# Adding the window mask with VectorE instead of a mask matmul, in a kernel of causal attention and six local-attention layers

## The chip, the cores and the metric

The kernel runs on one core of one Trainium2 chip. The metric is the device time of one execution in microseconds. PE is TensorE (PEld its weight loads), DVE is VectorE, ACT is ScalarE, POOL is GpSimd, SP the queue that issues the DMAs. A matmul writes into one of eight banks of PSUM (here `ps[0]` to `ps[7]`); DVE and ACT read the banks, POOL works in SBUF ("memory" below) alone.

## The reference, cut to what matters

A causal attention block is followed by six layers of local attention, each with a feed-forward block. The change touches only the softmax of the local attention, 8 batches of 512 tokens with 16 heads of 64 columns, in windows of 32 queries that look at 64 keys:

```python
sim = jnp.einsum('bhwie,bhwje->bhwij', bq, bk2) * QK_SCALE
sim = jnp.where(mask, -jnp.finfo(sim.dtype).max, sim)
attn = jax.nn.softmax(sim, -1)
out = jnp.einsum('bhwij,bhwje->bhwie', attn, bv2)
```

The mask depends on the position in the window, and it is another one for the first window of a sequence, which has no window before it.

## The kernel before

Every engine has its own instruction stream, written out by hand; they meet only at semaphores. The causal block comes first. Then each engine loops over the six layers. A layer's local attention runs over 32 tiles of 128 tokens (4 in each of 8 batches) as a software pipeline: `pipeline` calls `step` for t from 0 on, and in one step the parts of the work belong to different tiles, `lag` steps behind the newest (projection, squares and rotation lag 0, the transposes of q and k lag 1, scores and softmax lag 2, the transposed probabilities lag 3, weighing lag 3 and 4, the output projection up to lag 6). The feed-forward block follows after the last tile has drained.

A step has two halves, `wp` = 0 and 1. In a half the engines do, each strictly in this order:

- PE: `project(2wp)`, `turn_qk(2wp)`, `turn_p(wp)`, `project(2wp+1)`, `score(wp)`, in half 0 `windows`, then `weigh`, `turn_qk(2wp+1)`, `project_out`.
- ACT: `square(2wp)` (L777), `turned_qk(2wp)` and `turned_p(wp)` (copies, L668), `square(2wp+1)`, in half 0 two small copies, `weighed` (two copies), `turned_qk(2wp+1)`, `exp(wp)` (L820), `norms(wp)` (L786, L789, L793, which end with `rn`).
- DVE: `sums` (L1129, L1131), `rotate(2wp)` and `rotate(2wp+1)` (L1093), `shift(wp)` (L1116, L1119), two `square_sums` (L1105), then one of `update` and `rests_of_tile` (half 0) or `load_next` (half 1).
- POOL: two `scale` (L1311), `normalise` (L1320), two `add` (L1297).

What holds a half together: `rotate(c)` waits for `square(c)`; `add(c)` waits for `rotate(c)`; `norms` waits for the second `square_sums`; the first `square` of the next half stands behind `norms` in ACT's order; `scale` waits for `rn`. A tile of scores (128 x 512, the bank `sbank`) is made by 16 small matmuls of `score`. Ahead of them stands one matmul that puts the mask there: `identb` (the unit matrix) times `lmask`, both bfloat16, 128 x 512, and the scores are accumulated on top. `score` also waits until `shift` of the half before has read the bank for the last time (semaphore `sub`). `shift` takes the maximum of each head's 64 scores from the bank (L1116), waits for it, and subtracts it while it moves the scores to memory, into `dd` (L1119). `exp` works in place on `dd`.

Of the kernel before, what the change touches and what calls it, by code (L numbers as in the profile page):

```python
# [22 lines left out]
ALU = mybir.AluOpType  # L23
AX = mybir.AxisListType

P = 128
# [4 lines left out]
DEPTH, D, WIN = 6, 64, 32  # L31
HP = HEADS // 2
# [57 lines left out]
def build(nc, ins, out, layers=DEPTH):  # L90
    ctx = ExitStack()
    with ctx:
        def sb(name, shape, dt=F32):
            return ctx.enter_context(nc.sbuf_tensor("sb_" + name, [P] + shape, dt))

        def sem(name):
            return ctx.enter_context(nc.semaphore("s_" + name))
# [9 lines left out]
        identb = sb("identb", [P], BF16)  # L107
        lmask = sb("lmask", [2, HP * 2 * WIN], BF16)
# [21 lines left out]
        smax, ssum, srec = sb("smax", [2, HP]), sb("ssum", [2, HP]), sb("srec", [2, HP])  # L130
# [4 lines left out]
        def take(*shape):  # L135
            n = int(np.prod(shape))
            v = area[:, at[0]:at[0] + n]
            at[0] += n
            if len(shape) == 1:
                return v  # L140
            names = " ".join("abcde"[:len(shape)])
            return v.rearrange(f"p ({names}) -> p {names}", **dict(zip("abcde", shape)))
# [4 lines left out]
        dd, pT = take(2, 512), take(2, 512)  # L147
# [3 lines left out]
        kT = take(HP, WIN + T)  # L151
# [48 lines left out]
        def ea(h, qt, k0, k1):  # L200
# [7 lines left out]
        pj, rbank, sbank, tbank, ybank, mbank = ps[0:2], ps[2], ps[3], ps[4], ps[5:7], ps[7]  # L208

        S = {n: sem(n) for n in (  # L210

            "const", "xload0", "xload1", "xload2", "xload3", "c_weights", "eps_set", "v16_zero", "wo_zero", "w_loaded", "w_loaded2", "w1_loaded", "w2_loaded",
            "wcomb_mm", "wcomb_ready",

            "ln0_mean", "ln0_sq", "ln0_rstd", "ln0_x", "xn_tr", "xT_ready", "xs_zero",

            "xb_ready", "c_proj", "c_rope", "c_rope_part", "v_mm", "v_ready", "qm_ready", "c_score", "c_max",
            "c_exp", "c_split", "stack0", "stack1", "stack2", "stack3", "c_rec", "c_p", "c_tr", "c_ptev", "c_pv", "yT_ready", "ca_mm", "res_in", "ca_sum", "ca_out",

            "kT_zero", "w_split", "w_split_h", "w_split_a", "rots_ready", "wvo_mm", "wvo_ready", "xs_part", "xs_high", "xs_ready",  # L220
            "proj", "sq", "rotd", "ssq", "ssq_raw", "guard_set", "ln_part", "rn", "add", "qn", "tr", "ev", "score",
            "smax", "sub", "exp", "ssum", "srec", "pn", "pt", "ptev", "yy", "yev0", "yev1",
            "xwt", "xwev", "oo", "xupd",

            "lx", "lx_zero", "lmean", "ldif", "lsq", "lvar", "lln", "lrs", "lmul", "xn", "mhi", "mlo", "gate", "gelu", "aa",
# [17 lines left out]
        def behind(t, i, part, lag):  # L243

            s = t - lag
            if (part == 0 and s < 0) or (part == 2 and s >= 2 * TT):
                return None
            return s % TT, i + s // TT
# [106 lines left out]
        def _(pe):  # L355
            def mm(o, a, b, start=True, stop=True):
                return nc.tensor.matmul(o, a, b, start=start, stop=stop, skip_group_check=True)  # L357
# [84 lines left out]
            with pe.Fori(0, layers) as l:  # L442
# [14 lines left out]
                def step(t, i, part):  # L457
                    def g_of(bt):
                        return l * B + bt
# [47 lines left out]
                    def score(wp):  # L507
                        if not (v := behind(t, i, part, 2)):
                            return
                        tt, bt = v  # L510
                        pe.wait_ge(S["ev"], g_of(bt) * 16 + 4 * tt + 4)
                        pe.wait_ge(S["sub"], g_of(bt) * 8 + 2 * tt + wp)
                        first = tt == 0 and wp == 0
                        mm(sbank[:, :], identb[:, :], lmask[:, 0 if first else 1, :], True, False)
                        for g in range(HP):
                            for x in range(2):
                                hp, w = 2 * (g // 2) + x, wp + 2 * (g % 2)
                                k0 = tt * P + w * WIN
                                m = mm(sbank[64 * x:64 * x + 64, g * 64:(g + 1) * 64],
                                       qbd[:, tt % 2, hp, w, :, :].rearrange("p a b -> p (a b)"),  # L520
                                       kT[:, hp, k0:k0 + 2 * WIN], False, x == 1 and g == HP - 1)
                        m.then_inc(S["score"], 1)

                    def turn_p(wp):
# [66 lines left out]
                    for wp in range(2):  # L591
                        project(2 * wp)
                        turn_qk(2 * wp)
                        turn_p(wp)
                        project(2 * wp + 1)
                        score(wp)
                        if wp == 0:
                            windows()
                        weigh(4 - wp, 1 - wp)
                        turn_qk(2 * wp + 1)  # L600
                        project_out(wp)
# [327 lines left out]
        def _(dve):  # L929
            tt_, ts_ = nc.vector.tensor_tensor, nc.vector.tensor_scalar  # L930

            def bc(v, shape, axis):
                return v.unsqueeze(axis).to_broadcast(shape)
# [113 lines left out]
            with dve.Fori(0, layers) as l:  # L1047
# [28 lines left out]
                def step(t, i, part):  # L1076
                    def g_of(bt):
                        return l * B + bt
# [30 lines left out]
                    def shift(wp):  # L1109
                        if not (v := behind(t, i, part, 2)):  # L1110
                            return
                        tt, bt = v
                        m_ = g_of(bt) * 8 + 2 * tt + wp
                        dve.wait_ge(S["score"], m_ + 3)
                        s3 = sbank[:, :].rearrange("p (h k) -> p h k", h=HP)
                        nc.vector.tensor_reduce(smax[:, wp, :], s3, AX.X, ALU.max).then_inc(S["smax"], 1)  # L1116
                        dve.wait_ge(S["smax"], m_ + 1)
                        dve.wait_ge(S["pt"], m_ + 1)
                        tt_(dd[:, wp, :].rearrange("p (h k) -> p h k", h=HP), s3,  # L1119
                            bc(smax[:, wp, :], [P, HP, 64], 2), ALU.subtract).then_inc(S["sub"], 1)  # L1120

                    def sums(lag, wp):
                        if not (v := behind(t, i, part, lag)):
# [36 lines left out]
                    for wp in range(2):  # L1160
                        sums(3 - wp, 1 - wp)
                        rotate(2 * wp)
                        rotate(2 * wp + 1)
                        shift(wp)
                        square_sums(2 * wp)
                        square_sums(2 * wp + 1)
                        if wp == 0:
                            update()
                            if not (part == 0 and t == 0) and (v := behind(t, i, part, -1)):
                                rests_of_tile(*v)  # L1170
                        else:
                            load_next()
# [216 lines left out]
```

## Time and profile before

| | us |
|---|---|
| median of 3 runs (4154.02 to 4157.87) | 4154.56 |
| the profiled execution | 4155.47 |
| its span, first to last instruction | 4153.7 |
| busy: PE / PEld / DVE / ACT / POOL | 3814.5 / 2939.8 / 3258.6 / 3109.2 / 2498.3 |
| share of the span | 92% / 71% / 78% / 75% / 60% |
| mean granted TensorE clock | 0.971 of 2.4 GHz |

A matmul's end is modelled, so that a PE that is 92% busy isn't at its peak. The causal block fills the first 700 us, and the six layers take some 570 us each. In the last part of a layer, the feed-forward block, nothing of the change runs. A share over the whole span mixes these stages; the rows below are therefore read stage by stage.

### The profile page before, as it was taken

How to read it: one execution, taken by the hardware profiler on the slowest of the kernel's cores; microseconds unless marked ns; L12 is line 12 of the kernel's file. 1: busy time of each engine (PE TensorE's matmuls, PEld its weight loads, DVE VectorE, ACT ScalarE, POOL GpSimd, SP SyncE). 2: the span in 40 equal slices, each digit the busy share in tenths (PEclk: the TensorE clock that was granted, in tenths of full speed). 3: DMA queues.
4: the chain of work that ended last, by engine and by line, in shares of the span. 5: the costliest groups of instructions: out<-in, count | busy, mean ns of one | idle time of the engine just before them, and what ended most of it. 6: DMA issues, size and time to landing. Idle time of an engine off the chain costs nothing.

```text
span 4153.7 us, 101302 instructions
## 1 busy us (share of the span) xinstructions
PE 3814.5 (92%) x30950; PEld 2939.8 (71%) x31328; DVE 3258.6 (78%) x5635; ACT 3109.2 (75%) x7150; POOL 2498.3 (60%) x2247
## 2 busy tenths in 40 slices
PE   6999998899998999988999989999889999899998
PEld 4666665677766777766777667777667776677776
DVE  5877876888867888768888678887688886788876
ACT  4777776788866888857888668887578886688875
POOL 1221221777745777737777457776377774577763
PEclk9999999999998999998999989999989999999999
DMA  2111111000010000010000100000100000000002
GB/s 79 42 32 31 29 39 35 2 0 0 0 28 1 1 0 0 1 28 1 0 0 0 28 1 1 0 0 1 28 1 0 0 0 28 1 1 0 0 1 68
DMA packets 53261, 52.86 MB, mean 13 GB/s; under 512 B 13574, under 2 KB 40452, under 8 KB 51972
## 3 DMA queue, kind: packets, MB, share of 16 engines
q1 hardware_dynamic: 52996, 49.77, 4.5%
q8 instruction: 113, 1.85, 0.2%
q14 instruction: 152, 1.25, 0.1%
HBM read 28.77 MB, written 4.19 MB: 8 GB/s over the span
## 4 chain that ended last, share of the span: by engine, by line
issue 26%; PE 24%; ACT 24%; DVE 21%; ACTq 2%; DVEq 2%; POOL 1%; SPq 0%; DMA 0%; POOLq 0%
PE bank L357 19%; ACT sb_area L668 12%; DVE sb_ssq L1105 10%; DVE sb_smax L1116 6%; ACT sb_area L777 5%; PE bank L416 3%; ACT sb_lnb L786 3%; ACT sb_lnb L789 3%; DVE sb_area L1093 1%; PE bank L503 1%; POOL sb_area L1336 1%; DVE sb_nmx L1013 1%; DVE sb_area L1119 0%; PE bank L532 0%; DVE sb_area L1009 0%
## 5 line engine op out<-in xcount | busy, mean ns | idle before, releaser
L668 ACT ACTIVATE sb_area<-bank 128x512 f32<-128x512 f32 (+4 forms) x3029 | 1570.3, 553 | 259.0 <-PE bank L357 182.3
L357 PE MATMUL bank<-sb_area 128*64 128x64 f32 (+4 forms) x16624 | 1286.1, 274 | 94.9 <-issue 57.8
L1093 DVE TENSOR_TENSOR sb_area<-bank,sb_rots 128x1024 f32<-128x1024 f32 x768 | 939.2, 1224 | 395.2 <-ACT sb_area L777 394.4
L1311 POOL TENSOR_TENSOR sb_area<-sb_area,sb_rn 128x512 f32<-128x512 f32 x768 | 784.8, 1043 | 608.5 <-ACT sb_rn L793 608.5
L1297 POOL TENSOR_TENSOR sb_area<-sb_area 128x512 f32<-128x512 f32 x768 | 967.9, 1278 | 78.3 <-DVE sb_area L1093 76.2
L357 PEld LDWEIGHTS bank<-sb_area 128*64 128x64 f32 (+2 forms) x16624 | 849.5, 151 | 200.6 <-issue 139.1
L357 PE MATMUL bank<-sb_wqk_hi,sb_xwin 128*128 128x512 f32 x1536 | 729.7, 477 | 53.9 <-DVE sb_xwin L1073 43.6
L357 PE MATMUL bank<-sb_area,sb_wvo 128*128 128x256 f32 x3072 | 728.3, 381 | 3.1 <-DVE sb_xT L1151 3.1
L357 PEld LDWEIGHTS bank<-sb_area,sb_wvo 128*128 128x128 f32 x3072 | 555.0, 190 | 78.3 <-issue 12.8
L503 PE MATMUL bank<-sb_ident,sb_area 128*128 128x128 f32 x3072 | 494.9, 285 | 33.4 <-ACT sb_area L668 31.0
L503 PEld LDWEIGHTS bank<-sb_ident,sb_area 128*128 128x128 f32 x3072 | 358.8, 144 | 227.6 <-issue 160.0
L1105 DVE TENSOR_REDUCE sb_ssq<-sb_area 128x8 f32<-128x512 f32 x768 | 486.7, 675 | 0.0
L777 ACT ACTIVATE sb_area<-bank 128x512 f32<-128x512 f32 x768 | 460.4, 600 | 30.9 <-PE bank L357 14.5
L1320 POOL TENSOR_TENSOR sb_area<-sb_area,sb_srec 128x512 f32<-128x512 f32 x384 | 400.3, 1042 | 88.4 <-DVE sb_srec L1131 88.4
L1270 POOL TENSOR_TENSOR sb_ptT<-sb_xwin,sb_hm 128x512 fp32r<-128x512 f32 x128 | 137.8, 1077 | 510.8 <-PE bank L357 494.1
L722 ACT ACTIVATE sb_area<-bank,sb_nmx 128x128 f32<-128x128 f32 (+3 forms) x512 | 270.1, 528 | 178.5 <-DVE sb_nmx L1013 175.6
L357 PEld LDWEIGHTS bank<-sb_wqk_hi,sb_xwin 128*128 128x128 f32 x1536 | 304.2, 198 | 111.3 <-issue 48.9
L1013 DVE TENSOR_REDUCE sb_nmx<-bank 128x1 f32<-128x128 f32 (+3 forms) x512 | 249.1, 487 | 125.4 <-PE bank L357 114.4
L357 PE MATMUL bank<-sb_wqk_lo,sb_xwin 128*128 128x512 f32 x768 | 315.4, 411 | 0.0
L820 ACT ACTIVATE sb_area<-sb_area 128x512 f32<-128x512 f32 x384 | 242.9, 633 | 76.4 <-DVE sb_area L1119 70.9
L357 PE MATMUL bank<-sb_xwin,sb_ptT 128*128 128x128 f32 (+3 forms) x512 | 286.9, 561 | 13.3 <-POOL sb_ptT L1270 8.4
L1129 DVE TENSOR_REDUCE sb_ssum<-sb_area 128x8 f32<-128x512 f32 x384 | 261.6, 681 | 45.2 <-ACT sb_area L820 40.0
(103 smaller groups left out, 4861.7 us busy)
## 6 DMA issues: line engine op xcount, KB each, us to landing
sb_xwin<-sb_p SPq DMA_DIRECT2D x256, 64.0 KB, 2.0
sb_area<-in_Wqkv SPq DMA_DIRECT2D x7, 1024.0 KB, 5.8
sb_area<-in_WvT SPq DMA_DIRECT2D x7, 512.0 KB, 7.3
sb_wo_bd<-in_Wo SPq DMA_DIRECT2D x14, 256.0 KB, 8.2
sb_area<-in_x SPq DMA_DIRECT2D x4, 512.0 KB, 5.7
sb_area<-in_x SPq DMA_DIRECT2D x8, 256.0 KB, 2.9
x_plus_causal<-sb_area SPq DMA_DIRECT2D x8, 256.0 KB, 2.3
out<-sb_area SPq DMA_DIRECT2D x8, 256.0 KB, 3.5
```

Source lines behind the costliest of these rows:

```text
L357: return nc.tensor.matmul(o, a, b, start=start, stop=stop, skip_group_check=True)
L503: m = nc.tensor.transpose(rbank[:, j * P:(j + 1) * P], qn[:, c, j * P:(j + 1) * P], ident[:, :])
L668: return nc.scalar.activation(o, i, ACT.Copy)
L722: nc.scalar.activation(ea(k // TT, qt, 0, (qt + 1) * P), ps[k % 3][:, 0:(qt + 1) * P], ACT.Exp, bias=nmx[:, k % 8:k % 8 + 1], accum_out=ls ...
L777: nc.scalar.activation(sqb[:, c % 2, :], pj[c % 2][:, :], ACT.Square).then_inc(S["sq"], 1)
L1013: nc.vector.tensor_reduce(nmx[:, k % 8:k % 8 + 1], ps[k % 3][:, 0:(k % TT + 1) * P], AX.X, ALU.max, negate=True).then_inc(S["c_max"], 1)
L1093: tt_(t12[:, c % 2, :, :].rearrange("p u (h d) -> p u h d", h=8), src, bc(rots[:, tt, s, :, :], [P, 2, 8, D], 2), ALU.mult).then_inc(S["ro ...
L1105: nc.vector.tensor_reduce(ssq[:, tt % 2, half, 8 * (c % 2):8 * (c % 2) + 8], sqb[:, c % 2, :].rearrange("p (h d) -> p h d", h=8), AX.X, AL ...
L1129: nc.vector.tensor_reduce(ssum[:, wp, :], d3, AX.X, ALU.add).then_inc(S["ssum"], 1)
L1297: pt_(qsum[:, c % 2, :].rearrange("p (h e d) -> p h e d", h=8, e=2), t12[:, c % 2, 0, :].rearrange("p (h e d) -> p h e d", h=8, e=2), swap ...
L1311: pt_(qn[:, c, :].rearrange("p (h d) -> p h d", h=8), qsum[:, c % 2, :].rearrange("p (h d) -> p h d", h=8), r, ALU.mult).then_inc(S["qn"], 1)
L1320: pt_(dd[:, wp, :].rearrange("p (h k) -> p h k", h=HP), dd[:, wp, :].rearrange("p (h k) -> p h k", h=HP), srec[:, wp, :].unsqueeze(2).to_b ...
```

## The change

The mask matmul goes, and the first score matmul of each 64 x 64 block starts its own accumulation. `shift` now has three operations of 128 x 512 elements in place of two. The first adds `lmask` (bfloat16, memory) to the bank and writes `dd` (float32, memory). The maximum is taken from `dd`, and the subtraction reads `dd` and writes `dd`. The wait for `pt` (that `dd`'s old content was transposed) comes ahead of the first of them. `score` waits for the new semaphore `masked` instead of `sub`.

```diff
@@ score (PE)
-                        pe.wait_ge(S["sub"], g_of(bt) * 8 + 2 * tt + wp)
-                        first = tt == 0 and wp == 0
-                        mm(sbank[:, :], identb[:, :], lmask[:, 0 if first else 1, :], True, False)
+                        pe.wait_ge(S["masked"], g_of(bt) * 8 + 2 * tt + wp)
...
                                        qbd[:, tt % 2, hp, w, :, :].rearrange("p a b -> p (a b)"),
-                                       kT[:, hp, k0:k0 + 2 * WIN], False, x == 1 and g == HP - 1)
+                                       kT[:, hp, k0:k0 + 2 * WIN])
@@ shift (DVE)
                         dve.wait_ge(S["score"], m_ + 3)
-                        s3 = sbank[:, :].rearrange("p (h k) -> p h k", h=HP)
-                        nc.vector.tensor_reduce(smax[:, wp, :], s3, AX.X, ALU.max).then_inc(S["smax"], 1)
+                        dve.wait_ge(S["pt"], m_ + 1)
+                        tt_(dd[:, wp, :], sbank[:, :], lmask[:, 0 if tt == 0 and wp == 0 else 1, :], ALU.add)\
+                            .then_inc(S["masked"], 1)
+                        dve.wait_ge(S["masked"], m_ + 1)
+                        d3 = dd[:, wp, :].rearrange("p (h k) -> p h k", h=HP)
+                        nc.vector.tensor_reduce(smax[:, wp, :], d3, AX.X, ALU.max).then_inc(S["smax"], 1)
                         dve.wait_ge(S["smax"], m_ + 1)
-                        dve.wait_ge(S["pt"], m_ + 1)
-                        tt_(dd[:, wp, :].rearrange("p (h k) -> p h k", h=HP), s3,
-                            bc(smax[:, wp, :], [P, HP, 64], 2), ALU.subtract).then_inc(S["sub"], 1)
+                        tt_(d3, d3, bc(smax[:, wp, :], [P, HP, 64], 2), ALU.subtract).then_inc(S["sub"], 1)
```

## Rows read from the trace of the kernel before

**Rows 1.** Chain of waits, two halves of the second layer: start, us, engine, line.

```profile
1403.49 0.69 DVE sb_smax L1116
...
1410.99 0.69 DVE sb_smax L1116
1411.70 0.06 DVE sb_area L1119
...
1412.31 1.28 DVE sb_ssq L1105 x2
...
1414.29 0.04 ACT sb_rn L793
...
1415.03 1.08 ACT sb_area L668 x2
1416.11 0.50 ACT sb_area L777
...
1417.77 0.69 DVE sb_smax L1116
```

**Rows 2.** Who waited for whom, 760 to 1176 us: us, times, longest.

```profile
DVE sb_area L1093 <- ACT sb_area L777: 56.9, 116, 1.1
ACT sb_lnb L786 <- DVE sb_ssq L1105: 29.4, 58, 0.6
...
ACT sb_area L668 <- PE bank L357: 21.1, 34, 0.9
```

**Rows 3.** Busy time by stretch: length, PE, PEld, DVE, ACT, POOL, granted clock, DMA.

```profile
760.00:1176.00 416.00, 397.24 (x3834) 321.35 (x3891) 353.79 (x562) 342.92 (x751) 320.44 (x292) 1.00 0.00 1
1304.00:1324.00 20.00, 13.08 (x79) 9.51 (x81) 14.28 (x19) 12.93 (x31) 16.20 (x15) 0.74 0.00 1
1180.00:1210.00 30.00, 28.53 (x247) 21.96 (x245) 9.74 (x18) 16.51 (x31) 6.92 (x7) 1.00 0.01 1
...
220.00:240.00 20.00, 16.42 (x100) 11.11 (x98) 14.58 (x37) 15.63 (x51) 4.16 (x4) 1.00 0.08 21
```

**Rows 4.** Timeline, DVE: first and last maximum of layer one's full pipeline.

```profile
753.58 0.68 DVE L1116 TENSOR_REDUCE sb_smax<-bank 128x8 f32<-128x512 f32 x1
...
1176.12 0.68 DVE L1116 TENSOR_REDUCE sb_smax<-bank 128x8 f32<-128x512 f32 x1
```

**Rows 5.** Lines by themselves: min/median/max ns, first and last start.

```profile
L1119 DVE TENSOR_TENSOR sb_area<-bank,sb_smax x384: 690/691/693, 754.3 to 4049.1; 128x512 f32<-128x512 f32 x192
L1116 DVE TENSOR_REDUCE sb_smax<-bank x384: 678/680/694, 753.6 to 4048.4; 128x8 f32<-128x512 f32 x192
L1129 DVE TENSOR_REDUCE sb_ssum<-sb_area x384: 672/681/687, 756.3 to 4051.1; 128x8 f32<-128x512 f32 x192
L1093 DVE TENSOR_TENSOR sb_area<-bank,sb_rots x768: 1211/1224/1226, 728.0 to 4026.5; 128x1024 f32<-128x1024 f32 x192
L984 DVE TENSOR_TENSOR sb_area<-sb_area x16: 680/682/693, 47.8 to 594.2; 128x512 f32<-128x512 f32 x16
L1219 DVE TENSOR_TENSOR sb_p<-sb_area,sb_p x36: 691/692/1466, 1244.6 to 4127.2; 128x512 fp32r<-128x512 f32 x36
```

**Rows 6.** Timeline, PEld: the mask's weights and the first ones of the scores.

```profile
1407.39 0.10 PEld L357 LDWEIGHTS bank<-sb_lmask,sb_identb 128*128 128x128 bf16 x1 [0.27 <-issue]
1407.72 1.01 PEld L357 LDWEIGHTS bank<-sb_area 128*64 128x64 f32 x32 [0.23 <-issue]
```

**Rows 7.** Timeline, DVE and POOL, feed-forward block: a lengthened operation and its surroundings.

```profile
1243.22 2.32 POOL L1343 TENSOR_TENSOR sb_xwin<-sb_area,sb_xwin 128x512 fp32r<-128x512 f32 x2 [6.12 <-ACT sb_xwin L668]
...
1244.62 1.46 DVE L1219 TENSOR_TENSOR sb_p<-sb_area,sb_p 128x512 fp32r<-128x512 f32 x1
```

**Rows 8.** Timeline, POOL: the two adds of half 0 and of half 1.

```profile
1410.09 2.51 POOL L1297 TENSOR_TENSOR sb_area<-sb_area 128x512 f32<-128x512 f32 x2
...
1417.59 2.52 POOL L1297 TENSOR_TENSOR sb_area<-sb_area 128x512 f32<-128x512 f32 x2
```

**Rows 9.** Timeline, DVE: a maximum while the pipeline drains.

```profile
1192.13 0.69 DVE L1116 TENSOR_REDUCE sb_smax<-bank 128x8 f32<-128x512 f32 x1 [1.02 <-PE bank L357]
```

More of the change, by code:

```diff
@@ L221, in build @@
             "proj", "sq", "rotd", "ssq", "ssq_raw", "guard_set", "ln_part", "rn", "add", "qn", "tr", "ev", "score",
-            "smax", "sub", "exp", "ssum", "srec", "pn", "pt", "ptev", "yy", "yev0", "yev1",
+            "masked", "smax", "sub", "exp", "ssum", "srec", "pn", "pt", "ptev", "yy", "yev0", "yev1",
             "xwt", "xwev", "oo", "xupd",
```

## The prediction

> **What bounds the kernel now.** The change lies in the local attention alone, so I looked for that stage first, and in it for the resource whose lengthening lengthens a half. The busy shares point at PE: in the full pipeline of the first layer it is busy for 397.24 of 416 us, against 353.79 for DVE [rows 3]. A matmul's end is modelled, though, so I went on to the chain of waits. There a half runs through DVE and ACT alone [rows 1]: maximum at 1410.99, subtraction at 1411.70, the square sums at 1412.31, ACT's three norm operations ending with `rn` (starts 1414.29), the first square, two copies (1415.03), the second square (1416.11), the second rotation, and the next maximum at 1417.77. This is a closed loop: DVE waits for the square, ACT waits for the square sums. Third, the waits confirm it [rows 2]: in the 416 us DVE waits 56.9 us for the square (116 times, about twice per half), and ACT waits 29.4 us for the square sums (58 times, once per half). ACT also waits 21.1 us for PE, 34 times, but that is for the weighed values, which stand ahead of its wait for the square sums, so there is slack behind it. No row has the loop waiting for the scores in steady state.
>
> A half lasts 7.50 us (1403.49 to 1410.99) or 6.78 us (1410.99 to 1417.77), 14.28 for a step [rows 1]. As a check over the stage: 60 maxima, the first at 753.58 and the last at 1176.12, give 422.54/59 = 7.16 us [rows 4]. The 60 are the halves of steps that still have new tiles; with six layers there are 360 such halves (180 steps), and 24 more (4 a layer) while the pipeline drains, 384 in all, the count of L1116 [rows 5].
>
> **The change part by part.**
>
> *The mask matmul goes.* From its weights (1407.39) to the first ones of the scores (1407.72) it takes 0.33 us of PE's queue [rows 6]. PE isn't in the loop, so in the 360 full halves this is worth 0; it merely gives PE some room. In the drain it is otherwise: PE is busy for 28.53 of 30 us, DVE for 9.74 [rows 3], and the maximum there waits 1.02 us for PE [rows 9]. There PE sets the pace. I count 18 of the 24 halves (the first of a layer's four still hangs on the loop) with 0.33 us, about -6 us. The bounds are -8 (24 x 0.33) and +17 (24 x 0.71, if DVE's new operation shows after all).
>
> *One more DVE operation (add).* It reads the bank and memory and writes 128 x 512 float32, which is L1119's form, 691 ns [rows 5]. The bfloat16 operand is the one difference and no row has it; I take the same time. The maximum has to wait for its result, and the nearest pair of that kind is maximum and subtraction, 0.71 us from start to start (1410.99 to 1411.70) [rows 1]. So the loop grows by 0.71 us in each half. Nothing hides it: it stands between rotation and square sums, both in the loop. The wait for `pt`, moved ahead, costs nothing, since in PE's order `turn_p` stands before `score`. The early release of the bank through `masked` is worth nothing either, as `score` doesn't wait for it. Behind DVE's new wait for `masked` stands only work that needed the maximum, or follows it, already.
>
> *Maximum and subtraction from memory.* The maximum costs the same: 680 ns from the bank (L1116) and 681 from memory (L1129) [rows 5]. The subtraction by itself is 691 ns from bank and memory (L1119) and 682 from memory twice (L984). That would be 0.01 us gained, taken as 0.
> The Trainium skill would expect more from this part: VectorE: DVE Perf Modes, "The TRN2 errata", has a fixed 120 cycles of 0.96 GHz for a bank source and 58 for memory. An estimate from that page is 62 cycles, 0.065 us, for each of two operations in 360 halves, 47 us less. The rows of this case differ (1 and 9 ns).
>
> *But the subtraction now has two operands in memory, and POOL is at work then.* This is the part that decides the size. In the feed-forward block L1219, with two operands in memory, takes 691 ns at best and 692 in the median but 1466 at most [rows 5]. The long one starts at 1244.62 while POOL has two operations from 1243.22 to 1245.54 [rows 7]. It lasts 1.46 us and so ends at 1246.08, 0.54 us behind POOL. Read as one mechanism: such an operation does its first 0.15 us or so (0.69 - 0.54), then stands until POOL's running operation is over, and then takes its 0.54. Operations with one operand in the bank never do so: L1119 (690 to 693 ns) and L1093 (1211 to 1226 ns) keep their time in all their executions [rows 5], though the maximum at 1410.99 and L1119 behind it lie right under POOL's adds. Nor does the reduction from memory (L1129, 672 to 687).
> Where does the new subtraction fall? It starts at the old maximum's place plus twice 0.71. In half 0: 1410.99 + 1.42 = 1412.41, and POOL's adds end at 1410.09 + 2.51 = 1412.60 [rows 1, 8]. Stall: 0.19 - 0.15, 0.04 us. In half 1: 1417.77 + 1.42 = 1419.19, and the adds end at 1417.59 + 2.52 = 1420.11. Stall: 0.92 - 0.15, 0.77 us. POOL's sequence of five operations starts when `rn` is done and is over 5.8 us after `rn`'s start (1414.29 to 1420.11), so a longer loop doesn't move it against DVE: the stall comes back in each step. Together 0.81 us a step.
> The Trainium skill says the same in its GPSIMD Engine Reference, "Specifications": the SBUF interfaces are shared with VectorE, with contention for DVE instructions that have two SBUF inputs. This rule speaks against the change, and the trace agrees, by the 1466 ns above.
>
> *Sum.* Per step 14.28 + 2 x 0.71 + 0.81 = 16.51 us, that is 2.23 more; 180 steps make +401. With the drain's -6 it is +395, on the profiled execution's 4155.5: 4550 us. That execution stands 0.9 us above the median, so against the median the forecast is 4549; I give 4550.
>
> **The rivals.**
>
> *A: no stall.* The subtraction's second operand is only 8 values per partition, each repeated 64 times, and no row shows such an operation beside a busy POOL. If it is exempt, only the add remains: 360 x 0.71 - 6 = +250, 4405 us. For it: that gap in the rows, and that L1219 is stretched in few of its 36 executions (median 692), although few of them need have met POOL. Against it: the full second of POOL ahead of it in half 1.
>
> *B: PE loses its clock and becomes the bound.* PE's work per step is 397.24/416 of 14.28 us, less 0.66 for the two mask matmuls: 13.0 us, while the step grows to 16.5, so it is busy for four fifths. In the filling pipeline, where it was busy for 13.08 of 20 us, the granted clock was 0.74, a mixture of its two levels 1.2 and 2.4 GHz; in the causal block with 16.42 of 20 it was 1.00 [rows 3]. The new state lies near the second. PE would decide from a mean clock of 13.0/16.5 = 0.79 downwards; at 0.74 a step would take 13.0/0.74 = 17.6 us, and the whole 4155.5 + 180 x (17.6 - 14.28) = 4753 us. Against it: a slower clock makes PE busier again. Single dips are taken up by the slack.
> The Trainium skill, TensorE: Matmul & The Clock Gate, Part 1, also has a clock that follows how busy PE was.
>
> *C: not slower, since PE is the real bound.* The mechanism: PE, 95% busy, has no more slack than the loop, and the loop has at least 0.71 us of slack in a half that the chain of waits doesn't show. Then the add disappears and the matmul's 0.33 us come off all 384 halves: -127, 4029 us. It decides from a slack of 0.71 + 0.33 us a half. Against it: a chain that passes from DVE to ACT and back with handovers of some 0.05 us, and scores that are never waited for in the steady state.
>
> **How the numbers follow.** Forecast 4550 us with 0.73; A (4405) 0.15; B and other growth above 4640 0.07; C 0.04; 0.01 for something between. The forecast's own range is 4500 to 4620: it goes up by 54 us if the subtraction needs its full 0.69 us after POOL in every half (360 x 0.15), and down by the estimate that the operations from memory are a little faster or the stall in half 1 is partly missed. To leave out no more than 2 in 10, the range has to reach A: 4395 to 4640. That leaves out B and C, 0.11, and the tails of the rest. 0.2% (8 us) is about what a measurement can tell from no change. Faster by more than that: C, 0.03; within it 0.01, a loop slack that just takes up the add; slower 0.96.
>
> **What the profile would show.** Right: the mean of L1119's successor well above 0.69 us, in two groups (near 0.7 in one half, near 1.45 in the other); the add near 0.69; the step at 16.5 us; POOL's adds ending just as the long subtractions go on; PE's busy share in the stage near 80%, clock near 1; the chain still in DVE and ACT. A: all subtractions 0.68 to 0.69, step 15.7. B: clock of the stage under 0.85 and PE in the chain. C: a step of 14 us with maxima that wait for PE. The forecast would be wrong if the subtraction slipped between POOL's two adds, or if POOL's own operations were held by it and pushed on what waits for them.

## The result and the profile after

The changed kernel takes 4582.11 us (median of 4 runs, 4580.28 to 4583.36) against 4156.22 us for the kernel before (4 runs): the ratio is 1.1024, with a 95% interval of 1.1005 to 1.1043. It is 426 us slower; +395 was forecast. The profiled execution of the changed kernel has a span of 4580.6 us.

First the changed lines by themselves (min/median/max ns, first and last start). L1114 is the add, L1118 the maximum, L1120 the subtraction:

```profile
L1114 DVE TENSOR_TENSOR sb_area<-bank,sb_lmask x384: 650/681/692, 755.3 to 4475.6; 128x512 f32<-128x512 f32 x192
...
L1118 DVE TENSOR_REDUCE sb_smax<-sb_area x384: 686/686/690, 756.0 to 4476.3; 128x8 f32<-128x512 f32 x192
...
L1120 DVE TENSOR_TENSOR sb_area<-sb_area,sb_smax x384: 691/818/1795, 756.7 to 4477.0; 128x512 f32<-128x512 f32 x192
```

Add and maximum take about what was expected, 681 ns for the add instead of 691 and 686 for the maximum instead of 681. The subtraction, 690 to 693 ns before [rows 5], now goes up to 1795. The timeline of one step shows which ones (start, us, engine, line). Half 0 first, then half 1:

```profile
1495.68 2.53 POOL L1297 TENSOR_TENSOR sb_area<-sb_area 128x512 f32<-128x512 f32 x2
...
1498.01 0.74 DVE L1120 TENSOR_TENSOR sb_area<-sb_area,sb_smax 128x512 f32<-128x512 f32 x1
...
1503.96 2.51 POOL L1297 TENSOR_TENSOR sb_area<-sb_area 128x512 f32<-128x512 f32 x2
...
1504.14 0.68 DVE L1114 TENSOR_TENSOR sb_area<-bank,sb_lmask 128x512 f32<-128x512 f32 x1
...
1504.86 0.69 DVE L1118 TENSOR_REDUCE sb_smax<-sb_area 128x8 f32<-128x512 f32 x1
...
1505.58 1.44 DVE L1120 TENSOR_TENSOR sb_area<-sb_area,sb_smax 128x512 f32<-128x512 f32 x1
```

In half 0 POOL's adds end at 1498.21, and the subtraction ends at 1498.75, 0.54 us later. In half 1 they end at 1506.47, and the subtraction, which starts at 1505.58, ends at 1507.02, 0.55 us later. L1219 had shown 0.54 us in the feed-forward block before [rows 7]. This isn't one step alone: 274 of the 384 subtractions take more than 0.72 us, and each of them ends 0.55 us behind an operation of POOL. From the start of the add to that of the maximum, and from there to the subtraction, it is 0.72 us each in half 1.

The chain of waits of the same stretch (start, us, what) is the old loop with the add in it; the 0.83 us of "issue" stand for the held subtraction:

```profile
1504.14 0.69 DVE sb_area L1114
...
1506.11 0.83 issue
1506.94 1.28 DVE sb_ssq L1103 x2
1508.24 0.32 ACT sb_lnb L784
...
1513.02 0.69 DVE sb_area L1114
```

Busy time in the full pipeline (columns as in [rows 3]), to be held against its first line:

```profile
760.00:1176.00 416.00, 361.79 (x3286) 286.30 (x3288) 359.38 (x535) 294.57 (x648) 275.66 (x251) 0.93 0.00 0
```

PE is down from 397.24 to 361.79 us and its clock from 1.00 to 0.93. It now waits for ACT's copy ahead of the window transposes, as one line of the waits of that stretch says (us in total, times, longest). Before, the time of this wait was 7.0 us there.

```profile
PEld bank L559 <- ACT sb_area L666: 54.6, 23, 4.4
```

Where the 426 us are: I took the start of every subtraction. In the full pipeline of a layer, 60 of them now lie 8.31 us apart in the mean (8.30 to 8.32 over the six layers); before it was 7.16 in each. That is 6 x 59 x 1.15 = 407 us. From the last full one to the layer's last one (the drain, four halves) it took 20.75 us before and now takes 22.9 to 24.3 us, together +16 us. The rest, 3 us, is spread.

### The profile page after: what moved, and what is told of

Same layout as the page of the kernel before. It is cut to its first block, busy times and chain, and to the rows that moved or that the text cites. A ratio compares the mean times of both kernels' runs of the same rounds, so it can differ in the third digit from the quotient of the medians.

```text
span 4580.6 us, 101212 instructions
## 1 busy us (share of the span) xinstructions
PE 3957.4 (86%) x30944; PEld 3010.4 (66%) x30944; DVE 3667.2 (80%) x6019; ACT 3108.0 (68%) x7150; POOL 2501.5 (55%) x2247
## 4 chain that ended last, share of the span: by engine, by line
PE 30%; issue 24%; DVE 22%; ACT 18%; DVEq 1%; ACTq 1%; POOL 1%; SPq 0%; DMA 0%; POOLq 0%
PE bank L357 24%; DVE sb_ssq L1103 9%; ACT sb_area L666 9%; DVE sb_smax L1118 4%; DVE sb_area L1114 4%; ACT sb_area L775 4%; PE bank L416 3%; PE bank L503 2%; ACT sb_lnb L787 2%; ACT sb_lnb L784 2%; POOL sb_area L1336 1%; DVE sb_area L1091 1%; PE bank L559 1%; DVE sb_nmx L1011 1%; PE bank L530 1%
## 5 line engine op out<-in xcount | busy, mean ns | idle before, releaser
L357 PE MATMUL bank<-sb_area 128*64 128x64 f32 (+4 forms) x16624 | 1344.8, 282 | 33.3 <-ACT sb_area L666 19.9
L357 PEld LDWEIGHTS bank<-sb_area 128*64 128x64 f32 (+2 forms) x16624 | 878.1, 155 | 262.0 <-issue 180.9
L357 PE MATMUL bank<-sb_area,sb_wvo 128*128 128x256 f32 x3072 | 782.5, 401 | 3.1 <-DVE sb_xT L1151 3.1
L357 PE MATMUL bank<-sb_wqk_hi,sb_xwin 128*128 128x512 f32 x1536 | 732.7, 478 | 57.9 <-DVE sb_xwin L1071 43.8
L357 PEld LDWEIGHTS bank<-sb_area,sb_wvo 128*128 128x128 f32 x3072 | 600.1, 206 | 93.5 <-issue 12.8
L503 PE MATMUL bank<-sb_ident,sb_area 128*128 128x128 f32 x3072 | 532.9, 301 | 27.8 <-ACT sb_area L666 19.3
L503 PEld LDWEIGHTS bank<-sb_ident,sb_area 128*128 128x128 f32 x3072 | 384.1, 152 | 246.9 <-issue 175.4
L559 PE MATMUL bank<-sb_ident,sb_xs 128*128 128x128 f32 x384 | 95.9, 337 | 403.4 <-ACT sb_area L666 403.4
L1120 DVE TENSOR_TENSOR sb_area<-sb_area,sb_smax 128x512 f32<-128x512 f32 x384 | 404.0, 1052 | 13.3
L357 PEld LDWEIGHTS bank<-sb_wqk_hi,sb_xwin 128*128 128x128 f32 x1536 | 305.7, 199 | 116.2 <-issue 49.9
L559 PEld LDWEIGHTS bank<-sb_ident,sb_xs 128*128 128x128 f32 x384 | 42.3, 154 | 431.4 <-ACT sb_area L666 430.4
```

The source lines that it names most:

```text
L503: m = nc.tensor.transpose(rbank[:, j * P:(j + 1) * P], qn[:, c, j * P:(j + 1) * P], ident[:, :])
L1120: tt_(d3, d3, bc(smax[:, wp, :], [P, HP, 64], 2), ALU.subtract).then_inc(S["sub"], 1)
```

## The experiments

Ratios are against the kernel before, from runs on the same chip. It took 4155.7 to 4157.4 us there, so that times of different runs can be compared to about 2 us.

**One: the operands back in the bank.** The add writes into the bank, and what follows reads it there:

```diff
-                        tt_(dd[:, wp, :], sbank[:, :], lmask[...], ALU.add).then_inc(S["masked"], 1)
+                        tt_(sbank[:, :], sbank[:, :], lmask[...], ALU.add).then_inc(S["masked"], 1)
...
-                        nc.vector.tensor_reduce(smax[:, wp, :], d3, AX.X, ALU.max).then_inc(S["smax"], 1)
+                        nc.vector.tensor_reduce(smax[:, wp, :], s3, AX.X, ALU.max).then_inc(S["smax"], 1)
...
-                        tt_(d3, d3, bc(smax[:, wp, :], [P, HP, 64], 2), ALU.subtract).then_inc(S["sub"], 1)
+                        tt_(d3, s3, bc(smax[:, wp, :], [P, HP, 64], 2), ALU.subtract).then_inc(S["sub"], 1)
```

(`s3` is the bank; `score` waits for `sub` again.)

> The changed kernel, but the add writes its result back into the bank, and the maximum and the subtraction read the bank: three operations on VectorE as before, each with one operand in the bank. Theory (the subtraction is held by GpSimd because both its operands are in memory): the subtraction returns to 0.69 us in both halves, the stall of 0.75 us a step goes, 4582 - 180 x 0.75 = 4447 us. Rival (the length of the subtraction has to do with its place in the order, not with where its operands lie): it stays long, 4582 us.

Measured: 4423.78 us (4422.59 to 4425.89), ratio 1.0642 (1.0624 to 1.066). The add costs 267 us with no stall, and putting the subtraction's operand in memory another 158. That is more than the 135 in the expectation: the stall was 0.84 us a step rather than 0.75 (see below), and the drain gets shorter too, to 20.84 us in five of the six layers. The subtraction and the add by themselves:

```profile
L1121 DVE TENSOR_TENSOR sb_area<-bank,sb_smax x384: 690/691/693, 755.5 to 4316.6; 128x512 f32<-128x512 f32 x192
...
L1114 DVE TENSOR_TENSOR bank<-bank,sb_lmask x384: 673/690/700, 754.0 to 4315.1; 128x512 f32<-128x512 f32 x192
```

POOL's adds (1488.42 to 1490.93) run over this subtraction too, in the step below, and leave its length alone:

```profile
1488.42 2.51 POOL L1298 TENSOR_TENSOR sb_area<-sb_area 128x512 f32<-128x512 f32 x2
...
1490.05 0.69 DVE L1121 TENSOR_TENSOR sb_area<-bank,sb_smax 128x512 f32<-128x512 f32 x1
```

**Two: the same collision taken away from POOL's side.** VectorE is as in the changed kernel; the adds take a quarter of the columns, 0.46 us instead of 1.28:

```diff
-                        pt_(qsum[...], t12[:, c % 2, 0, :]..., swapped, ALU.add)
+                        pt_(qsum[...][:, 0:2], t12[:, c % 2, 0, :]...[:, 0:2], swapped[:, 0:2], ALU.add)
```

> The changed kernel with GpSimd's adds over the first 128 of 512 columns alone; the other columns of the rotated q and k keep old values, so that part of the computation is left out. Nothing of VectorE is changed. Theory: GpSimd is done long before the subtraction starts, which then takes 0.69 us in both halves: about 4447 us, and if the kernel before had been given the same cut it would have stayed at 4156, since GpSimd isn't in its loop. Rival (the subtraction is long for a reason of its own): 4582 us.

Measured: 4423.94 us (4421.98 to 4426.81), ratio 1.064 (1.0623 to 1.0658). Two edits on different engines bring the same time, to 0.2 us. All but 6 of the 384 subtractions are short, with both operands in memory:

```profile
L1120 DVE TENSOR_TENSOR sb_area<-sb_area,sb_smax x384: 691/692/1443, 759.3 to 4319.1; 128x512 f32<-128x512 f32 x192
```

That shows that the length isn't the operation's own. The kernel before with the same cut wasn't run.

**Three: the mask matmul alone.**

```diff
-                        mm(sbank[:, :], identb[:, :], lmask[:, 0 if first else 1, :], True, False)
...
```

(The score matmuls start their own accumulation, as in the changed kernel.)

> The kernel before without its mask matmul and with nothing in its place, so the masking is left out. Theory (TensorE isn't in the loop): 4156 us less 6 us of the drain, 4148 to 4156. Rival C (TensorE is the bound): 384 x 0.33 us less, 4029 us. A third case, that TensorE's idle time lets its clock fall: a little above 4156.

Measured: 4155.13 us (4153.63 to 4159.44), ratio 0.9995 (0.9986 to 1.0005). Rival C falls: nothing clear of noise is gained by relieving PE. Per half the pipeline keeps 7.16 us, and only the drain gets shorter, 20.10 instead of 20.75 us a layer, 4 us in all.

**Four: work for PE, to keep its clock.**

```diff
                         pe.wait_ge(S["masked"], g_of(bt) * 8 + 2 * tt + wp)
+                        for _ in range(3):
+                            mm(sbank[:, :], identb[:, :], lmask[:, 1, :])
```

> The changed kernel with three matmuls of identb times lmask in the bank ahead of each tile of scores, whose result the scores overwrite: TensorE gets some 0.7 to 1 us more work in a half and waits that much less. Theory (in the changed kernel TensorE waits for ScalarE's copy ahead of the window transposes, its clock falls, and the slow matmuls behind it lengthen some steps by what is left over beside add and stall, 0.13 us a step, and the drain): the clock of the pipeline goes from 0.94 towards 1, 4582 - 24 - 15 = 4543 us. Rival (the rest of 0.13 us has another source): 4582 us, or more, since TensorE has more to do.

Measured: 4583.54 us (4577.94 to 4586.09), ratio 1.1022 (1.1004 to 1.104): no gain. The granted clock did rise, from 0.93 to 0.98 in the pipeline (760 to 1180 us):

```profile
760.00:1180.00 420.00, 376.34 (x3440) 287.20 (x3491) 364.43 (x542) 298.96 (x656) 279.22 (x253) 0.98 0.00 0
```

My expectation failed. The steps take 16.63 us in the mean with the higher clock and 16.65 with the lower. So the clock lengthens a step by 0.02 us at most. The drain got longer (24.9 us a layer in five of six, against 22.9 in four of the changed kernel's): PE sets the pace there, and the three matmuls cost it 0.65 us a half (the last two halves of a layer take 5.55 and 5.15 us instead of 4.90 and 4.51).

**Five to eight: the new work taken out of the loop.** If the loop is rotation, maximum, subtraction, square sums, norms, squares, then another order on two engines shortens it:

```diff
@@ VectorE
-                        shift(wp)
                         square_sums(2 * wp)
                         square_sums(2 * wp + 1)
+                        shift(wp)
@@ ScalarE
+                        norms(wp)
                         exp(wp)
-                        norms(wp)
```

In the kernel before:

> The kernel before with one change of order: on VectorE the two square sums come ahead of maximum and subtraction, and on ScalarE the norms come ahead of exp. Theory (the loop is rotation, maximum, subtraction, square sums, norms, squares): maximum and subtraction, 0.71 + 0.61 us a half, leave the loop, which would then be some 11.7 us a step, and the next limit sets the pace: TensorE, whose work in a step (of 14.34 us in the mean) is 13.6 to 14.2 us. So 4157 - 180 x (0.1 to 0.7): 4030 to 4139 us. Rival (the loop is not what sets the pace): 4157 us or above, since exp comes later.

Measured: 4139.25 us (4133.76 to 4139.63), ratio 0.9953 (0.994 to 0.9967). This is 18 us below the kernel before, at the upper edge of what I had expected (4030 to 4139), and 443 below the changed one. The loop no longer sets the pace; the chain of waits now consists of PE alone (by line, 1420 to 1450 us):

```profile
by line: PE bank L357 77.1%; PE bank L503 13.6%; PE bank L532 7.3%; PE bank L561 2.5%
```

and yet VectorE is busy for 406.36 of 416 us, where it was busy for 353.79 [rows 3]:

```profile
760.00:1176.00 416.00, 408.79 (x3922) 323.58 (x3922) 406.36 (x566) 344.31 (x755) 328.13 (x293) 0.99 0.00 1
```

The reason is the same collision in other places. The copies of the next tile and the tile's residue, which fell into POOL's idle time before, now meet its scales. (The residue is what rounding left of the tile, L1073, a subtraction with both operands in memory.) By themselves, in this order:

```profile
L1065 DVE COPY sb_xs<-sb_xT x192: 206/890/1059, 728.1 to 3986.7; 64x128 f32 x144, 64x128 f32<-64x128 f32 x48
...
L1073 DVE TENSOR_TENSOR sb_xwin<-sb_xs,sb_xwin x192: 279/953/1103, 728.9 to 3994.5; 128x128 fp32r<-128x128 f32 x192
```

In the changed kernel:

> The changed kernel with the same order: square sums first, norms ahead of exp. Theory: add, maximum and subtraction leave the loop. VectorE's work in a step, 13.5 us and the stall, becomes the limit, and the subtraction now stands 3.8 us behind the start of the second rotation, where GpSimd has started its scales, so that it is held there again, by up to one of their 1.04 us in each half: 15.3 us a step with 0.5 us of stall a half, 4330 us; 14.3 us a step, 4150 us, if it finds GpSimd idle. Rival (the place of the new work in the order doesn't matter): 4582 us.

Measured: 4601.35 us (4596.55 to 4607.03), ratio 1.1065 (1.1048 to 1.1082): slightly slower than the changed kernel, and well above what I had expected (4150 to 4330). The subtractions are held at POOL's scales in both halves (1.11 and 1.23 us in the mean):

```profile
L1120 DVE TENSOR_TENSOR sb_area<-sb_area,sb_smax x384: 691/1245/1582, 759.2 to 4501.6; 128x512 f32<-128x512 f32 x192
```

That is 0.95 us a step over 2 x 0.69, no more than expected. What I had left out are the copies and the residue, which are held here too: in the first layer's pipeline they take 1.06, 0.29 and 0.84 us in the mean instead of 0.21, 0.22 and 0.28. These 1.5 us on top of the expected 15.3 give the step that was measured, 16.86 us. The rule has another side as well: 19 subtractions start 0.03 to 0.09 us ahead of a scale of POOL. They keep their 0.69 us, and the scale takes 1.51 to 1.57 us instead of 1.04.

With the operands in the bank (edit one) and this order:

> As the kernel with the add in the bank (its subtraction has one operand in the bank), with the same order: square sums first, norms ahead of exp. Theory: no stall wherever the subtraction falls, so the limit is VectorE's work of 13.5 us plus its waits or TensorE's 13 to 13.5 us: 14.0 to 14.8 us a step, 4100 to 4240 us. What it lies below the changed kernel with this order is what the meeting with GpSimd costs there. Rival (no effect of the operand's place once the order is changed): the same time as that one.

Measured: 4341.36 us (4339.07 to 4343.03), ratio 1.0445 (1.0429 to 1.0461), 100 us above the top of what I expected, but 260 below the one just told. So the operand's place decides here too, and more than in the first order (158). VectorE is busy for 398.41 of 416 us, and a step takes 15.4 us. Here too copies and residue are held, for 1.2 us a step (0.23, 0.98 and 0.67 us in the mean), which the expectation lacked. That VectorE's own work sets the pace is read from its share alone; the chain of waits still passes through DVE and ACT.

And without mask matmul, from the kernel before in this order:

> The kernel before without its mask matmul (the masking is left out), with the order changed: square sums first, norms ahead of exp. Theory (with the loop shortened TensorE is the limit): now the mask matmul's 0.33 us of each half count, up to 180 x 0.66 = 119 us below the kernel before in that order. Rival (TensorE is not the limit there either, but VectorE or ScalarE is): the same time as the kernel before in that order.

Measured: 4132.91 us (4126.28 to 4134.61), ratio 0.9936 (0.9921 to 0.9952), 6 us below the same order with it, hardly clear of noise; up to 119 had been expected. The share of VectorE, 407.35 of 416 us, suggests why: with PE relieved, VectorE and its held operations are next. Runs nine and ten test that.

**Nine and ten: the held operations moved.** On top of the new order, copies and residue go between maximum and subtraction, where POOL is idle; they leave their old place behind it.

```diff
                         nc.vector.tensor_reduce(smax[:, wp, :], s3, AX.X, ALU.max).then_inc(S["smax"], 1)
+                        if wp:
+                            load_next()
+                        elif v := behind(t, i, part, -1):
+                            rests_of_tile(*v)
...
```

> The kernel before with the changed order (square sums first, norms ahead of exp) and one step more: the two copies of the next tile (L1065, L1066, 0.89 and 0.99 us instead of 0.21 and 0.22 in that order, because they now meet GpSimd) and the residue of the tile (L1073, 0.95 instead of 0.28) go between maximum and subtraction, where GpSimd is idle for about 0.7 us. Theory (these operations too are held by GpSimd, and VectorE is then nearly full): they return to about 0.2 to 0.3 us and VectorE's share falls from 98% to some 90%; the time falls only as far as TensorE lets it, 0 to 20 us below that order, 4119 to 4139 us. Rival (their length has nothing to do with where GpSimd is): they stay long and the time is 4139 us.

Measured: 4145.35 us (twelve executions, eleven of them 4142.92 to 4149.75 and one 4202.21), ratio 0.9986 (0.9964 to 1.0009). This is 6 us above what I expected (4119 to 4139). Their lengths do return:

```profile
L1065 DVE COPY sb_xs<-sb_xT x192: 205/208/668, 725.1 to 3987.9; 64x128 f32 x144, 64x128 f32<-64x128 f32 x48
...
L1073 DVE TENSOR_TENSOR sb_xwin<-sb_xs,sb_xwin x192: 278/280/480, 725.9 to 3995.4; 128x128 fp32r<-128x128 f32 x192
```

and VectorE is busy for 353.94 of 416 us instead of 406.36. The time doesn't fall, it rather rises a little (a step takes 14.25 us in both orders): PE sets the pace there, and it doesn't profit.

> The same without the mask matmul (the masking is left out). Theory: with the held operations of VectorE gone and TensorE relieved of 0.66 us a step, neither is full any more, and the time falls clearly below the 4133 us of the order without mask matmul: 13.5 to 13.9 us a step, 4020 to 4100 us. Rival: 4133 us, if something else sets the pace.

Measured: 4115.32 us (4113.23 to 4117.9), ratio 0.9902 (0.9887 to 0.9916). This is 18 us below run eight and 30 below run nine. So relieving PE alone gained 6 us and relieving VectorE alone nothing, but both together 24: the two were level. It is still less than I had expected (4020 to 4100). The chain there is mixed (1420 to 1450 us), with 30.5% in PE's L357 and the rest spread over ACT and DVE; what holds it at this time wasn't followed further.

## Why the prediction was right, and where its sizes were off

*The bound.* That the loop through DVE and ACT sets the pace, and not the busier PE, was right. Run three shows it from one side (0 us for 0.33 us of PE work in each half) and run five from the other: the loop shortened, PE takes over at once, 18 us further down. PE was thus close behind the loop, which the forecast had not priced but which couldn't change the sign: relieving PE alone brought nothing.

*The add.* Forecast 0.71 us a half and 256 in all. Run one, which has the add without the stall, has steps of 15.81 us against 14.34 in the mean: 1.47 for two halves, 180 x 1.47 = 265 us, of 267 measured. The pairs are 0.72 us apart instead of 0.71, which makes 1.44 of the 1.47 us; the remaining 0.03 us a step wasn't followed.

*The stall.* Forecast 0.04 us in half 0, 0.77 in half 1, 0.81 a step. In run four, where all subtractions of half 1 were held, they took 0.76 and 1.46 us in the mean, 0.07 and 0.77 over their 0.69: 0.84 a step. In the changed kernel it is 0.07 and 0.68, since in 20 of the 180 steps the subtraction of half 1 comes a microsecond later, meets only the last 0.06 to 0.18 us of POOL's add and takes 0.69 to 0.72 us. Such steps are not shorter for it (16.8 us against 16.6). What delays them wasn't followed; in run four, with the higher clock, none is late. As a price, runs one and two give 158 us where 146 were forecast; some 14 of the 158 lie in the drain, where no stall was forecast (126.4 us over the six layers in run one, 140.4 in the changed kernel). Rival A, with its open question whether 8 repeated values count as an operand in memory, is answered: they do. The Trainium skill, GPSIMD Engine Reference, "Specifications", names contention with VectorE instructions that have two SBUF inputs. The trace agrees: 274 of 384 subtractions are held in the changed kernel, and none in run one. The Trainium skill, VectorE: DVE Perf Modes, "The TRN2 errata", gives a source in memory a smaller fixed cost than one in a bank. That doesn't show here: the maximum took 680 ns from the bank [rows 5] and takes 686 from memory.

*The drain.* This term was the worst sized, and it is the larger part of the missing 31 us: -6 us were forecast, and it became +16. The removed matmul is worth 4 us there (run three). But the first of a layer's four halves, which still hangs on the loop, was priced at nothing, and PE's wait and its clock weren't priced at all. The four halves of a layer's drain took 4.06, 6.85, 5.11 and 4.72 us before; they take 4.78, 8.8 (10.0 in two layers), 4.90 and 4.51 in the changed kernel. The add alone does little: in run one the drain is 20.84 us in five layers, 0.1 above the kernel before. With the held subtractions PE waits longer for ACT's copy, and its clock is low when it goes on (PEld, changed kernel, start of the second half):

```profile
1251.47 0.22 PEld L559 LDWEIGHTS bank<-sb_ident,sb_xs 128*128 128x128 f32 x2 [3.60 <-ACT sb_area L666]
1252.01 1.36 PEld L357 LDWEIGHTS bank<-sb_area 64*128 64x128 f32 x8 [0.33 <-issue]
```

The same eight weight loads in the kernel before:

```profile
1181.14 0.73 PEld L357 LDWEIGHTS bank<-sb_area 64*128 64x128 f32 x8 [0.17 <-issue]
```

After 3.60 us of waiting the eight weight loads take 1.36 us instead of 0.73. The granted clock from 1246 to 1256 us is 0.83, and 1.00 in the 10 us on either side. What the clock alone costs can be read in run one, whose second half of the drain appears at either level with the same work (columns as in [rows 3]; first layer, then third):

```profile
1225.47:1234.27 8.80, 8.80 (x75) 6.83 (x76) 2.97 (x5) 5.23 (x10) 2.91 (x3) 0.81 0.00 0
2456.59:2463.97 7.38, 7.36 (x75) 5.68 (x76) 2.98 (x6) 5.14 (x10) 2.91 (x3) 1.00 0.00 0
```

That is 1.4 us at a granted clock of 0.81. In the changed kernel this half has 0.81 in four layers (8.8 us) and 0.70 in two (10.0 to 10.1), in none 1.00. If it too would take 7.4 us at 1.00, the clock's part is 4 x 1.4 + 2 x 2.7 = 11 of the 16 us, an estimate. No run changes the clock of the drain alone.

*Rival B* had the right sign and little more: the clock fell to 0.93 in the pipeline, well above the 0.79 from which PE would have decided, and lifting it back (run four) brought 0.02 us a step. Where PE does decide, in the drain, the clock costs those 11 us.

## What to carry to other kernels

Before moving work to VectorE, find the closed loop that sets the pace and see whether the new operation stands in it; a chain of waits that goes around without PE outweighs PE's 95% busy share. An operation of VectorE with two operands in memory, or a copy within memory, must be placed against GpSimd's timeline; one operand left in the bank makes it free of that. A new order that takes work out of the loop is cheap to try, but it moves every other operation against GpSimd too.

## What the runs showed of the hardware

An operation of VectorE on 128 x 512 float32 with both inputs in memory that starts while GpSimd works ends 0.54 to 0.55 us behind the end of GpSimd's running instruction, whatever is left of it (0.74 and 1.44 us long instead of 0.69 in the step above, up to 1.79). All 274 held subtractions of the changed kernel do so. This holds also if one input is only 8 values a partition, each repeated 64 times. The smaller operations end earlier behind it: in run five the held copies of 64 x 128 float32 within memory (0.21 us alone, 0.89 in the median) 0.08 us, the held residues (0.28 alone, 0.95 in the median) 0.15 us. In all three cases it is the operation's own length less 0.13 to 0.14 us. If VectorE starts first, by as little as 0.03 us, GpSimd's operation is the one that is held (1.51 to 1.57 us instead of 1.04, run six). Maxima from memory are not held (686 to 690 ns in the changed kernel, most of them beside a working GpSimd). VectorE can add in place in a bank for 690 ns, against 681 into memory.
